# Two images' attention mixing in one group of column tiles, with the heads of one image exchanged

## What is computed

```python
scores = jnp.einsum('biph,biqh->biqp', k, q)
mask = jnp.tril(jnp.ones((s, s), dtype=scores.dtype))
scores = jnp.tril(scores) - 10000000000.0 * (1.0 - mask)
attn = jax.nn.softmax(scores / np.sqrt(D_HEAD), axis=-1)
z = jnp.einsum('biph,biqp->biqh', v, attn)
```

## Time and profile before

| | |
|---|---|
| three runs, median | 270.75 us |
| the profiled execution's own time | 271.7 us |
| its span, first to last instruction | 269.9 us |
| granted TensorE clock | 1.0 of full speed throughout the span |
| busy: matmul / VectorE / ScalarE / GpSimd | 251.7 / 212.7 / 172.6 / 83.8 us |
| mixing (L729) | 384 matmuls, 25.8 us busy, mean of one 280 ns |
| turnings (L717) | 192 matmuls, 29.4 us busy, mean of one 277 ns |
| chain that ended last | TensorE 57%, VectorE 30%, ScalarE 6% |

### The profile page before, as it was taken

The page is one execution under the profiler, slowest core; times in us unless marked ns, Lnnn a source line. Parts: engine busy times, 40 slices in busy tenths (PEclk is TensorE's granted clock), DMA queues, the critical chain, the costliest instruction groups (busy, mean ns, idle before and its releaser), DMA issues.

```text
span 269.9 us, 4613 instructions
## 1 busy us (share of the span) xinstructions
PE 251.7 (93%) x1545; PEld 184.6 (68%) x1547; DVE 212.7 (79%) x542; ACT 172.6 (64%) x490; POOL 83.8 (31%) x151
## 2 busy tenths in 40 slices
PE   7999879699998998989999899999899999999994
PEld 2777557465776566666576666788678878888883
DVE  3675669965599797997979957397699969599985
ACT  2276344698676856768667697675485587567760
POOL 5100104988894762946724220000400000000000
PEclk9999999999999999999999999999999999999999
DMA  7800000014222020000000000041101000531101
GB/s 219 323 2 2 0 1 0 0 29 130 80 78 79 8 73 2 0 2 0 0 5 0 0 2 2 24 134 43 38 32 47 2 0 0 170 99 48 39 0 39
DMA packets 9318, 11.84 MB, mean 44 GB/s; under 512 B 704, under 2 KB 5952, under 8 KB 9168
## 3 DMA queue, kind: packets, MB, share of 16 engines
q1 hardware_dynamic: 8864, 11.23, 13.7%
q10 hardware_dynamic: 432, 0.33, 0.4%
HBM read 11.00 MB, written 0.56 MB: 43 GB/s over the span
## 4 chain that ended last, share of the span: by engine, by line
PE 57%; DVE 30%; ACT 6%; issue 4%; POOL 2%; DMA 1%; DVEq 0%; SPq 0%; ACTq 0%
PE bank L717 5%; PE bank L729 5%; PE bank L693 5%; PE bank L665 5%; DVE negmax L1083 5%; PE bank L959 4%; PE bank L960 4%; PE bank L962 4%; PE bank L947 4%; PE bank L949 3%; PE bank L948 3%; DVE probT L1142 3%; DVE hlo L1337 2%; DVE ht L1049 2%; DVE stats L1035 2%
## 5 line engine op out<-in xcount | busy, mean ns | idle before, releaser
L479 ACT ACTIVATE prob<-bank,negmax 128x256 f32<-128x256 f32 (+1 forms) x128 | 52.5, 425 | 17.1 <-DVE negmax L1083 16.7
L606 ACT ACTIVATE hb<-bank,pk 128x512 f32<-128x512 f32 x64 | 42.8, 708 | 17.8 <-PE bank L949 17.8
L1337 DVE TENSOR_TENSOR hlo<-hb,hhi 128x512 fp32r<-128x512 f32 x64 | 42.7, 689 | 11.9 <-ACT hhi L609 10.8
L1083 DVE TENSOR_REDUCE negmax<-bank 128x2 f32<-128x512 f32 (+1 forms) x48 | 32.6, 686 | 13.1 <-PE bank L699 12.6
L717 PE MATMUL bank<-pk,prob 128*128 128x128 f32 x192 | 29.4, 277 | 2.2 <-ACT prob L479 1.7
L344 POOL TENSOR_TENSOR rstd<-ve,neghalf 128x2 f32<-128x2 f32 x16 | 11.5, 729 | 58.4 <-DVE ve L1044 58.4
L479 ACT ACTIVATION_READ_ACCUMULATOR prob<-bank,negmax 128x1 f32 x128 | 26.6, 208 | 0.0
L717 PEld LDWEIGHTS bank<-pk,prob 128*128 128x128 f32 x192 | 22.0, 142 | 6.3 <-ACT prob L479 3.6
L729 PE MATMUL bank<-probT,vh 128*32 128x128 f32 x384 | 25.8, 280 | 0.1
L947 PE MATMUL bank<-xhi,w_hi 128*128 128x512 f32 x64 | 25.4, 397 | 0.2
L959 PE MATMUL bank<-hhi,w_hi 128*128 128x512 f32 x64 | 25.3, 395 | 0.0
(11 more groups left out here) (149 smaller groups left out, 503.3 us busy)
## 6 DMA issues: line engine op xcount, KB each, us to landing
w_raw<-w SPq DMA_DIRECT2D x16, 256.0 KB, 3.1
comb_b<-routes SPq DMA_DIRECT2D x16, 256.0 KB, 3.4
pk<-packed SPq DMA_DIRECT2D x1, 1408.0 KB, 8.6
pk<-packed SPq DMA_DIRECT2D x1, 560.0 KB, 5.6
xs<-x SPq DMA_DIRECT2D x3, 128.0 KB, 2.7
out<-acc SPq DMA_DIRECT2D x3, 128.0 KB, 1.7
xs<-x ACTq DMA_DIRECT2D x1, 128.0 KB, 2.9
out<-acc ACTq DMA_DIRECT2D x1, 128.0 KB, 1.7
```

The lines of the kernel that those rows point to most:

```text
L479: last = nc.scalar.activation(prob[n][:, u % 2, i * width:(i + 1) * width], lane[n][u % 2][:, i * width:(i + 1) * width], ACT.Exp, bias=ne ...
L606: nc.scalar.activation(hb[blk % 2][:, j, :], h_bank[j][:, :], ACT.Relu, bias=bias).then_inc(h_ready, 1)
L1083: V.tensor_reduce(negmax[n][:, unit_query(u), heads[0]:heads[-1] + 1], lane[n][u % 2][:, :].rearrange("q (h k) -> q h k", h=len(heads)), A ...
L1337: V.tensor_tensor(hlo[blk % 2][:, j, :], hb[blk % 2][:, j, :], hhi[blk % 2][:, j, :].bitcast(F32), ALU.subtract).then_inc(hlo_ready, 1)
```

## The change

In the odd image of a pair the units of the later query tile (the wide ones) take the other two heads of their four: where the even image has heads 0, 1 the odd one has 2, 3, and so on. And TensorE's list has one mixing for both images, at the end of the step, behind both images' scores and turnings.

```diff
-        def unit_heads(u):
-            return SCORE_BANKS[u][1]
+        def unit_heads(n, u):
+
+            query, heads = SCORE_BANKS[u]
+            return [h ^ (2 * (n % 2)) for h in heads] if query == 1 else list(heads)
...
-            def mix(a, n, u):
-                pe.wait_ge(pT_ready[n], a * UNITS + u + 1)
+            def mix(a, ns, u):
+                for n in ns:
+                    pe.wait_ge(pT_ready[n], a * UNITS + u + 1)
                 key_tiles = unit_width(u) // 128
-                for kt in range(key_tiles):
-                    for i, h in enumerate(unit_heads(u)):
-                        g, r = divmod(h, HG)
-                        col = (2 * g + unit_query(u)) * 128
-                        at = (i * key_tiles + kt) * 128
-                        last = mm(lane[n][3][HP * r:HP * r + HP, col:col + 128], vh[n][:, kt, h, :],
-                                  probT[n][:, u % 2, at:at + 128],
-                                  start=(kt == 0), stop=(kt == key_tiles - 1), tile_position=(0, HP * r))
-                if u == UNITS - 1:
-                    last.then_inc(av_full, 1)
+                products = [(kt, i, n) for kt in range(key_tiles) for i in range(4 // key_tiles) for n in ns]
+                if key_tiles == 1:
+                    products.sort(key=lambda product: product[2])
+                for kt, i, n in products:
+                    h = unit_heads(n, u)[i]
+                    g, r = divmod(h, HG)
+                    col = (2 * g + unit_query(u)) * 128
+                    at = (i * key_tiles + kt) * 128
+                    last = mm(lane[n][3][HP * r:HP * r + HP, col:col + 128], vh[n][:, kt, h, :],
+                              probT[n][:, u % 2, at:at + 128],
+                              start=(kt == 0), stop=(kt == key_tiles - 1), tile_position=(0, HP * r))
+                    if u == UNITS - 1 and (kt, i) == (key_tiles - 1, 4 // key_tiles - 1):
+                        last.then_inc(av_full, 1)
...
                     if 1 <= u <= UNITS:
                         turn_probs(a, n, u - 1, aside)
-                    if u >= 2:
-                        mix(a, n, u - 2)
+                if u >= 2:
+                    mix(a, ns, u - 2)
```

More of the change, by code:

```diff
@@ L477, in exps @@
                 width = unit_width(u)
-                for i, h in enumerate(unit_heads(u)):
+                for i, h in enumerate(unit_heads(n, u)):
                     last = nc.scalar.activation(
@@ L688, in scores @@
                 width = unit_width(u)
-                i, heads = unit_query(u), unit_heads(u)
+                i, heads = unit_query(u), unit_heads(n, u)
                 dst = lane[n][u % 2]
@@ L1081, in largest @@
                 dve.wait_ge(s_full[n], a * UNITS + u + 1)
-                heads = unit_heads(u)
+                heads = unit_heads(n, u)
                 V.tensor_reduce(negmax[n][:, unit_query(u), heads[0]:heads[-1] + 1],
```

## The result

The changed kernel takes **269.68 us** as a median of 14 runs (267.93 to 271.12), the kernel before 270.72 in the runs beside them; the ratio is 0.9944, with a 95% interval of 0.9918 to 0.9969. The change is a gain of 1.0 us where 4.4 was forecast, and the median lies above the range of the prediction, which ended at 268.6. The spread has grown as well, from 1.2 to 3.2 us, and that is the first clue.

The account below looks back on a forecast made before the run. TensorE was taken to bind the first and last attention phases, VectorE the second. Savings of 2.1+0.5+0.66+1.1 = 4.4 us gave 267.3 from 271.7, or 266.4 as a median; own range 265.4 to 267.6, full range 265.2 to 268.6.

Parts of the forecast that it names:

- Step 2 nothing: Fourth attention phase, step 2: no gain, as one mixing of 0.56 was already hidden in the wait for `ht`.
- First phase: First attention phase, first scores to projections: 2.1 us saved, of 3.1 less 0.42 offered.
- The replay with its two waits for ScalarE: First phase stepped through from its trace rows: a step takes 3.06 us; waits for ScalarE cost 0.25 and 0.5.
- the price of a pair: Joint mixing of two images, sixteen matmuls in four rounds of four: 0.58 us to the next full-width matmul.
- Ends: Ends of attention phases, where both mixings already stand together: 0.5 us saved of 1.3, 0.1 of it in the first.
- Second and third phase: Middle attention phases: 0.33 us saved in each, from the feed-forward product starting sooner in step 3; VectorE binds from there.
- Fourth phase: Last attention phase: 1.1 us saved by an earlier last turning, and the router and experts follow TensorE.
- Faster: Whole kernel: chance 0.88 of a gain, made of the main forecast, the half-gain rival and a gain above 6 us.
- the same: Whole kernel within 0.5%, 1.35 us, of the time before: chance 0.09.
- B: Rival: matmuls of different images do not overlap, so a pair costs 1.00 us; 269.7 us; chance 0.08.
- C: Rival: the two images' banks exclude each other, a wide pair costs 2.0 us; about 10 slower, 281; chance 0.03.
- A: Rival: ScalarE and VectorE pass on half, 2.5 us of gain remain, 268.3 us; chance 0.10.

Follow-up runs that it names:

- one idle matmul: Changed kernel plus a single matmul with unread result ahead of the wait for normalized tokens in step 2 of the three later phases: 266.78 us, ratio 0.9839.
- unit 0 apart: Changed kernel with unit 0's mixing back at its old places, image by image, in the three later phases: 266.8 us, ratio 0.9868.
- move alone: Kernel before with unit 0's two mixings, each by itself, behind both turnings in the three later phases, old heads: 273.29 us, ratio 1.0073.
- two idle matmuls: Changed kernel plus two matmuls with unread results ahead of the wait for normalized tokens in step 2 of the later phases: 266.67 us, ratio 0.9841.
- four idle matmuls: Changed kernel plus four matmuls with unread results ahead of the wait for normalized tokens in step 2 of the later phases: 267.01 us, ratio 0.9862.
- changed, again: The changed kernel unaltered, run again for a second trace: 270.1 us, ratio 0.9969 against the kernel before.
- joint only: Changed kernel without the exchange of heads, joint mixing kept: 272.92 us, ratio 1.0063 without the slowest run.
- heads alone: Kernel before with only the exchanged heads, mixings at their old places: 270.55 us, ratio 0.9989.

## Why the prediction was wrong

**The term that failed** is "Step 2 nothing" with its reason, "The pair of unit 0 costs 0.58 behind the wait for `ht`, in which one mixing of 0.56 was hidden: nothing." For the queue of the changed kernel it is right: with one idle matmul the order is that of the change and the clock holds, and the three later phases take 26.70, 26.63 and 25.16 us, within 0.1 of unit 0 apart. What was not asked is what the moved mixing left behind. It had filled part of the wait; without it TensorE idles 1.8 to 2.0 us instead of 1.1 to 1.2, and in every one of 22 runs the granted clock fell at least once, at 1.4 to 1.6 us a fall. The prediction read the earlier trace rows, said that those waits do not get shorter, and never that they get longer. The granted clock stood at 1.00 in every window it read the earlier trace rows, and it gave no rival to the clock. The move alone, the idle matmuls and the mixing put back show this cause from three sides.

**The sum**, against the kernel in which the clock holds (unit 0 apart against before, from the table):
- First phase: 2.1 forecast, 2.08 measured. The replay with its two waits for ScalarE held, and so did the price of a pair, 0.58 against 0.57.
- Ends: 0.5 forecast, 0.30+0.16+0.17 = 0.63. The first was 0.3 instead of 0.1, though this stage takes 6.21 to 6.38 in the five traces of the table with four column groups, so 0.15 to 0.32.
- Second and third phase: 0.33 each forecast, 0.44 and 0.39. The product waits for VectorE's copy as it was read, and starts when that ends (the changed kernel, second phase):

```profile
87.97 0.69 DVE L1148 COPY probT<-bank 128x512 f32<-128x512 f32 x1
```

```profile
88.72 0.71 PE L655 MATMUL bank<-w_eff,hT 128*128 128x128 f32 x4
```

- Fourth phase: 1.1 forecast, 0.89.
- Together 4.47 (with 0.04 of the rest) against 4.4. In the medians, 266.8 against 270.85, it is 4.05; with two idle matmuls 266.67 against 270.63, 3.96. The 0.4 between the sum of single traces and the medians is not explained. The forecast of 266.4 describes these kernels and not the changed one.
- Two slips of arithmetic change nothing here. "Faster" adds up to 0.89, not 0.88, and "the same", 0.09, is more than the whole of B, 0.08. The steps of C add up to 10.3 to 12.7, of which "about 10" is the lower end.

**The rivals.** A did not happen. B was excluded by the windows, as the earlier trace rows had said, but its price was wrong: with the clock held, 271.4 and not 269.7, on the slower side. Its second and third phases were taken for 0.1 lost each and its fourth for even; they lose more (0.35 in the fourth, by the table), and the first gains less. C did not happen: a pair costs 0.57, not 2.0. The missing 3 us lay in none of them.

**The two rules.** That a weight load overlaps running matmuls only in another row group (the Trainium skill, TensorE: Matmul & The Clock Gate, "What overlaps and what doesn't") did not hold for column groups: in the window of 0.43 us shown above the profile has sixteen matmuls busy for 0.43 and sixteen loads for 0.33, so loads overlap matmuls although all use the same rows. The prediction had drawn from it that nothing would overlap, which is more than a rule on loads says. A rule that bears on what was missed stands on the same page of the Trainium skill (TensorE: Matmul & The Clock Gate, "Why this matters for your kernels"): avoid idle gaps between bursts of matmuls, or the clock goes back. The gaps that it warns of are longer than those here, of 1.8 to 2.0 us, behind at least one of which it fell in every run of the changed kernel. The measurement decides: gaps that this rule allows were too long in this kernel.

**A better version.** Unit 0 mixed apart, or one or two idle matmuls ahead of the wait, beat the changed kernel by about 3 us and the kernel before by 4. Their medians, 266.7 to 266.8, and that of four idle matmuls, 267.0, do not differ beyond their spread.

## What to carry to other kernels

A piece of work that is hidden in a wait costs nothing to run, but it may be what keeps TensorE's clock up: before it is moved out, or made faster, read how long the engine will be idle there, and fill that place or leave the piece in it. A spread that grows from run to run, with a mean granted clock below 1.00, points to this; the clock has to be read for every run and not from one profile, and the cost is read by comparing the same stage at both levels. Price a change of order for what leaves a wait as well as for what enters the path.

## What the runs showed of the hardware

- The granted clock fell behind idle stretches of 1.8 to 2.0 us in otherwise dense work, and stayed at half for about 3.4 us in each of the six falls that the traces hold. They began 1.1 us (changed), 1.5 and 1.5 (changed, again), 0.5 (move only), 1.2 and 0.0 us (joint only) after TensorE had started again.
- Idle stretches of 1.0 to 1.2 us went with a fall rarely: a mean clock of 0.994 in 3 of 52 runs of the kernel before, in 2 of 12 with the heads alone, in 1 of 6 with four idle matmuls and in none of 6 with unit 0 apart. None of the runs at 0.994 has a trace here, so where their clock fell is not known. With one idle matmul and idle stretches of about 1.6 to 1.8 us (estimated above) the mean clock was 0.997 to 1.00 in five runs.
- Which of the three waits is hit, and how many, changes from run to run of the same kernel: the two traces of the changed kernel show it (one fall, in the fourth phase; two, in the second and third), and by the mean clocks there are one to three in each of 22 runs.
- Matmuls in different groups of 32 columns overlap across two images and two banks even when they are listed image by image (heads only: 0.59 for sixteen, 1.00 before).
